# Eight shared groups moved beside the last sums, and rest tiles in a ring of six

## The reference

```
up_s   = einsum('th,seh->tse', xt, shared_up)            # 2 shared experts, 128 hidden
shared = einsum('tse,she->th', gelu(up_s), shared_down)
probs  = softmax(xt @ router_w.T);  topk_p, topk_i = top_k(probs, 4)   # of 16 experts
act    = gelu(einsum('th,reh->tre', xt, routed_up)) * gate
routed = einsum('tre,rhe->th', act, routed_down)
out    = x + shared + routed
```

## Time and profile before

| | us |
|---|---|
| median of 3 runs | 2615.87 (2613.97 to 2619.16) |
| the profiled execution: time | 2607.09 |
| its span | 2605.3 |
| PE / DVE / ACT / POOL busy in the span | 2062.6 / 1587.6 / 1255.6 / 1218.3 |
| SP's first load of the sums, last sum's store issued | 2350.8, 2601.9 |

### The profile page before, as it was taken

How to read it: one execution, slowest core, us unless ns; L and a number is a source line. 1 busy time by engine, 2 the same in 40 slices (tenths; PEclk the granted TensorE clock), 3 DMA queues, 4 the chain that set the end, 5 groups by cost and what they waited for, 6 DMA issues and landing times. The chain is left out here.

```text
span 2605.3 us, 55887 instructions
## 1 busy us (share of the span) xinstructions
PE 2062.6 (79%) x20646; PEld 1553.4 (60%) x20646; DVE 1587.6 (61%) x4387; ACT 1255.6 (48%) x2364; POOL 1218.3 (47%) x1648
## 2 busy tenths in 40 slices
PE   5889898989889898888888789999999998970000
PEld 3656565656666666666565567787778777760000
DVE  3566666666666666665666346666666666654666
ACT  3454544454545455454544346666666666650000
POOL 1034444444434443434444637777777767770000
PEclk8999999999999999999999799999999999995555
DMA  8254545545454545453544467777777777759999
GB/s 263 82 162 145 175 151 164 165 149 175 147 172 146 172 143 175 142 175 126 170 139 160 175 219 242 255 240 247 259 259 242 256 260 241 262 194 373 411 413 358
DMA packets 373934, 547.32 MB, mean 210 GB/s; under 512 B 100385, under 2 KB 306210, under 8 KB 369570
## 3 DMA queue, kind: packets, MB, share of 16 engines
q1 hardware_dynamic: 321634, 393.20, 46.5%
q0 software_dynamic: 52032, 150.54, 15.3%
HBM read 241.12 MB, written 302.52 MB: 209 GB/s over the span
## 5 line engine op out<-in xcount | busy, mean ns | idle before, releaser
L1050 POOL DMA_INDIRECT xs<-xn,idx x512 | 503.3, 983 | 601.9 <-DVE xn L907 157.7
L1075 POOL DMA_INDIRECT yt<-yo,ix x572 | 552.9, 967 | 225.7 <-issue 144.0
L671 ACT ACTIVATE pr<-A 128x512 f32<-128x512 f32 x512 | 264.4, 602 | 396.8 <-PE A L505 396.8
L802 DVE TENSOR_REDUCE ms<-A 128x4 f32<-128x512 f32 x512 | 316.6, 680 | 75.4 <-PE A L481 74.4
L627 PE MATMUL A<-wt,hh 128*128 128x256 f32 x1144 | 244.2, 296 | 0.7 <-DVE hl L952 0.7
L941 DVE TENSOR_TENSOR xl<-A,xh 128x512 fp32r<-128x512 f32 x286 | 183.3, 681 | 100.7 <-ACT xh L722 100.5
L585 PE MATMUL A<-ident,xr 128*128 128x128 f32 x1400 | 187.6, 278 | 63.5 <-DMA xr<-xs 31.1
L585 PEld LDWEIGHTS A<-ident,xr 128*128 128x128 f32 x1400 | 161.2, 142 | 115.6 <-DMA xr<-xs 42.9
L540 PE MATMUL A<-wos,ot 128*128 128x256 f32 x512 | 164.9, 450 | 79.8 <-ACT ot L680 79.8
L501 PE MATMUL A<-qt,km 32*128 32x128 f32 x4096 | 219.7, 333 | 0.6 <-DVE mt L822 0.6
L501 PEld LDWEIGHTS A<-qt,km 32*128 32x128 f32 x4096 | 183.9, 211 | 54.1 <-issue 49.8
(11 more groups left out here) (145 smaller groups left out, 4098.9 us busy)
## 6 DMA issues: line engine op xcount, KB each, us to landing
xr<-xs SPq DMA_DIRECT2D x143, 576.0 KB, 5.1
xs<-empty SPq DMA_DIRECT2D x36, 2048.0 KB, 10.7
gb<-yt SPq DMA_DIRECT2D x32, 2048.0 KB, 16.1
xb<-in_x SPq DMA_DIRECT2D x32, 512.0 KB, 6.6
cg<-in_ctx_t SPq DMA_DIRECT2D x32, 512.0 KB, 4.0
yd<-xb SPq DMA_DIRECT2D x32, 512.0 KB, 3.2
x2d<-xn SPq DMA_DIRECT2D x32, 512.0 KB, 3.0
xr<-x2d SPq DMA_DIRECT2D x32, 512.0 KB, 4.6
```

The lines of the kernel that those rows point to most:

```text
L671: ac(pr[:, 4 * b:4 * b + 4, :].rearrange("p h s -> p (h s)"), banks[4 + b][:, :], ACT.Exp, scale=SCALE)\
L802: v.reduce_max(ms[n % 2][:, b, 0:4], banks[b][:, :].rearrange("p (h t) -> p h t", h=4), AX.X)\
L1050: q.indirect_dma_start(xs, bass.IndirectOffsetOnAxis(ap=idx[:, n, k:k + 1], axis=0), x2[g % 4][:, i, :], None).then_inc(sent[g % 4], 16)
L1075: q.indirect_dma_start(yt, bass.IndirectOffsetOnAxis(ap=ix[:, n % 8, k:k + 1], axis=0), yo[n % 4][:, k, :], None).then_inc(put[n % 4], 16)
```

## The change

`LATE = 8`. The shared groups 24 to 31 are no longer spread between the routed blocks: they are the last eight units, behind block 142. The other 18 are spread anew, one after every seven or eight blocks.

The sums become steps of the same lists. `OPEN`, behind the down matmuls of the last block, waits for the scatters and the stores to `yd` and loads four `gb` and six `rr` tiles. `SUM` steps stand behind the down matmuls of each late group. They follow `ORDER`: 0, 1, 2, 3, 24, 4, 5, 25, 6, 7, 8, 26, 9, 10, 11, 27, 12, 13, 28, 14, 15, 16, 29, 17, 18, 19, 30, 20, 21, 31, 22, 23. A late group has no `yr` tile: DVE adds its down matmuls' result into the `rr` tile that its sum uses, and nothing is stored to `yd`. On DVE this add stands ahead of the sums of that step (two or three early groups and then its own). `rr` is a ring of six; `xr` is moved behind `xl` in memory, so that the six tiles lie over `wt`, `xh` and one `xl`, which the late groups don't use. SP loads the `rr` of place f + 5 behind a wait for the store of place f - 1.

```diff
+LATE = 8
-    rest = G - AHEAD
+    rest = G - AHEAD - LATE
...
-        while g < G and (g - AHEAD + 1) * NT <= (t + 1) * (rest + 1):
+        while g < G - LATE and (g - AHEAD + 1) * NT <= (t + 1) * (rest + 1):
...
-    return out
+    return out + [("S", n) for n in range(G - LATE, G)]
...
+ORDER = sorted(range(G), key=lambda g: ((g + 1) / (G - LATE) if g < G - LATE else (g - G + LATE + 1.5) / (LATE + 1), g))
...
             out.append(("DN", u - 1))
+            if UNITS[u - 1] == ("R", NT - 1):
+                out.append(("OPEN", 0))
+            if u - 1 >= NU - LATE:
+                upto = ORDER.index(UNITS[u - 1][1])
+                while done <= upto:
+                    out.append(("SUM", done))
+                    done += 1
...
+        rr = [es.enter_context(nc.sbuf_tensor(f"rr{k}", [P, GT, E], F32)) for k in range(6)]
...
-                if kind == "S":
+                if kind == "S" and n < G - LATE:
...
+            def OPEN(_):
+                for k in range(4):
+                    sp.wait_ge(put[k], 16 * GT * len(range(k, NT, 4)))
+                for k in range(2):
+                    sp.wait_ge(yr_kept[k], 16 * ((G - LATE) // 2))
+                for f in range(6):
+                    if f < 4:
+                        load_gathered(f)
+                    load_rest(f)
+
+            def SUM(f):
+                sp.wait_ge(added, f + 1)
+                sp.dma_start(token_rows(out, ORDER[f]), rr[f % 6][:, :, :]).then_inc(stored[f % 6], 16)
+                if f + 4 < G:
+                    load_gathered(f + 4)
+                if f > 0 and f + 5 < G:
+                    sp.wait_ge(stored[(f - 1) % 6], 16 * ((f - 1) // 6 + 1))
+                    load_rest(f + 5)
...
-                    dve.wait_ge(yr_in[n % 2], 16 * (n // 2 + 1))
+                    if n < G - LATE:
+                        y = yr[n % 2]
+                        dve.wait_ge(yr_in[n % 2], 16 * (n // 2 + 1))
+                    else:
+                        f = ORDER.index(n)
+                        y = rr[f % 6]
+                        dve.wait_ge(rr_in[f % 6], 16 * (f // 6 + 1))
```

More of the change, by code:

```diff
@@ L89, in ffn_steps @@
 def ffn_steps():
-    out, up = [], 0
+    out, up, done = [], 0, 0
     for u in range(-2, NU + 1):
@@ L103, in ffn_steps @@
             out.append(("DN", u - 1))
+            if UNITS[u - 1] == ("R", NT - 1):
[5 more added lines that the diff above has]
+                    done += 1
         if u + 2 < NU and UNITS[u + 2][0] == "R":
             out.append(("WC", UNITS[u + 2][1]))
-    return out
+    return out + [("SUM", f) for f in range(done, G)]
 ATT = attention_steps()
@@ L215, in sc @@
             return late.enter_context(nc.sbuf_tensor(name, shape, dt))
-        xr = [sc(f"xr{k}", [P, GT, W]) for k in range(3)]
         wt = [sc(f"wt{k}", [P, 2, 2, E], F32R) for k in range(3)]
@@ L220, in program @@
         xl = [sc(f"xl{k}", [P, KC, T], F32R) for k in range(2)]
+        xr = [sc(f"xr{k}", [P, GT, W]) for k in range(3)]
         xf = [sc(f"xf{k}", [P, KC, T]) for k in range(2)]
@@ L231, in program @@
         gb = [es.enter_context(nc.sbuf_tensor(f"gb{k}", [P, GT, TOPK, E], F32)) for k in range(4)]
-        rr = [es.enter_context(nc.sbuf_tensor(f"rr{k}", [P, GT, E], F32)) for k in range(4)]
+        rr = [es.enter_context(nc.sbuf_tensor(f"rr{k}", [P, GT, E], F32)) for k in range(6)]
         banks = [es.enter_context(nc.psum_tensor(f"A{b}", [P, 512], F32)) for b in range(8)]
@@ L255, in program @@
         put = [sem(f"put{k}") for k in range(4)]
-        gb_in, rr_in = [sem(f"gb_in{k}") for k in range(4)], [sem(f"rr_in{k}") for k in range(4)]
-        add_done, added, stored = sem("add_done"), sem("added"), [sem(f"stored{k}") for k in range(4)]
+        gb_in, rr_in = [sem(f"gb_in{k}") for k in range(4)], [sem(f"rr_in{k}") for k in range(6)]
+        add_done, added, stored = sem("add_done"), sem("added"), [sem(f"stored{k}") for k in range(6)]
         block = es.enter_context(nc.Block())
@@ L375, in DN @@
                     sp.dma_start(token_rows(yd, n), yr[n % 2][:, :, :]).then_inc(yr_kept[n % 2], 16)
-                    if 0 < n < G - 1:
+                    if 0 < n < G - LATE - 1:
                         sp.wait_ge(yr_kept[(n - 1) % 2], 16 * ((n - 1) // 2 + 1))
@@ L386, in TR @@
                     load_unit(u + 3)
[L388 to L396, removed]
-                             yt[g * P * GT * TOPK:(g + 1) * P * GT * TOPK, :].rearrange("(p r) e -> p (r e)", p=P))\
-                    .then_inc(gb_in[g % 4], 16)
@@ L400, in load_rest @@
[L400 to L413, removed]
@@ L414, in _, with load_gathered, load_rest @@
-            for k in range(4):
-                sp.wait_ge(stored[k], 16 * (G // 4))
+            def load_gathered(f):
+                g = ORDER[f]
+                sp.dma_start(gb[f % 4][:, :, :, :].rearrange("p i k e -> p (i k e)"),
+                             yt[g * P * GT * TOPK:(g + 1) * P * GT * TOPK, :].rearrange("(p r) e -> p (r e)", p=P))\
+                    .then_inc(gb_in[f % 4], 16)
+            def load_rest(f):
+                sp.dma_start(rr[f % 6][:, :, :], token_rows(yd, ORDER[f])).then_inc(rr_in[f % 6], 16)
@@ L417, in _ @@
+            run(FFN, {"TR": TR, "DN": DN, "OPEN": OPEN, "SUM": SUM})
+            for k in range(6):
+                sp.wait_ge(stored[k], 16 * len(range(k, G, 6)))
         @block.tensor
@@ L966, in DN, with SUM @@
                 else:
-                    dve.wait_ge(yr_in[n % 2], 16 * (n // 2 + 1))
+                    if n < G - LATE:
[5 more added lines that the diff above has]
+                        dve.wait_ge(rr_in[f % 6], 16 * (f // 6 + 1))
                     for k, b in enumerate(own):
                         wait_filled(dve, b, "DN", u)
-                        y2 = yr[n % 2][:, 2 * k:2 * k + 2, :].rearrange("p q e -> p (q e)")
+                        y2 = y[:, 2 * k:2 * k + 2, :].rearrange("p q e -> p (q e)")
                         v.tensor_tensor(y2, banks[b][:, :], y2, ALU.add).then_inc(drain[b], 1)
-            run(FFN, {"TR": TR, "U": U, "DN": DN})
-            for g in range(G):
-                p = g % 4
+            def SUM(g):
+                p, h = g % 4, g % 6
                 dve.wait_ge(gb_in[p], 16 * (g // 4 + 1))
-                dve.wait_ge(rr_in[p], 16 * (g // 4 + 1))
+                dve.wait_ge(rr_in[h], 16 * (g // 6 + 1))
+                if ORDER[g] >= G - LATE:
+                    u = UNITS.index(("S", ORDER[g]))
+                    for b in FFN_BANKS["DN"](u):
+                        wait_drained(dve, b, "DN", u)
                 pair = [gb[p][:, :, k:k + 2, :].rearrange("p i k e -> p i (k e)") for k in (0, 2)]
@@ L981, in _ @@
                 dve.wait_ge(add_done, 2 * g + 1)
-                v.tensor_tensor(rr[p][:, :, :], rr[p][:, :, :], gb[p][:, :, 0, :], ALU.add).then_inc(add_done, 1)
+                v.tensor_tensor(rr[h][:, :, :], rr[h][:, :, :], gb[p][:, :, 0, :], ALU.add).then_inc(add_done, 1)
                 dve.wait_ge(add_done, 2 * g + 2)
-                v.tensor_tensor(rr[p][:, :, :], rr[p][:, :, :], gb[p][:, :, 1, :], ALU.add).then_inc(added, 1)
+                v.tensor_tensor(rr[h][:, :, :], rr[h][:, :, :], gb[p][:, :, 1, :], ALU.add).then_inc(added, 1)
+            run(FFN, {"TR": TR, "U": U, "DN": DN, "SUM": SUM})
         @block.gpsimd
```

## The result

The changed kernel takes 2588.88 us (median of 6 runs, 2583.81 to 2594.46) against 2612.36 for the kernel before in the same comparison. The ratio is 0.9916, 95% interval 0.9895 to 0.9936: 17 to 27 us less. The forecast was 26.4 us less.

The account below looks back on a forecast made before the run. The prediction took GpSimd to bound the expert stretch and the DMA queue the last; -40 + 2.6 + 7 + 4 = -26.4 us, taken off the median 2615.87, gave 2589 us, with 8 in 10 in 2568 to 2610.

Parts of the forecast that it names:

- GpSimd bounds the expert stretch: Expert stretch: GpSimd, at 5.25 us a routed block, sets the pace despite TensorE's 91%; 143 blocks take 750.5 us.
- 40 us from the waits: Routed stretch: with eight groups gone, GpSimd's 54 us of waits shrink, gaining 40 us (bounds 17 and 54).
- a balance of 26.0 against 26.25 us between two five-block groups: Routed stretch: over five blocks and a shared group PE needs 26.0 us, GpSimd 26.25, leaving nothing for PE's load waits.
- The rival that gave the waits to the group itself: Routed stretch: PE's 9.2 us between outputs around a group makes GpSimd wait; gain only 3 us, 2613; chance 12%.
- the price of the six-block groups (0.73): Routed stretch: each of the 18 remaining groups costs GpSimd 0.73 us of waits, 13 us in all.
- Two moved loads, 2.6 us: Last stretch: two x2d loads of late groups stand behind the opening on SP, adding 2.6 us.
- The opening, 7 us: Start of the sums: DVE's first late add waits for rr tile 4, the queue empties about 7 us (bounds 4 and 10).
- Inside the ring, 4 us: Last stretch: late adds four places apart each leave the DMA queue empty 1 us, four times, adding 4 us.
- The ring of six gives nothing: Last stretch: the deeper ring of rest tiles adds no gain, because the DMA queue is already full.
- the rival that it makes the queue faster: Last stretch: the longer ring lifts the rate from 412 to 430 GB/s, 10 us less, 2579; chance 12%.
- PE's late work is hidden: Last stretch: PE's 15 us a late group fits into 3 or 4 sums, at least 22.9 us, adding nothing.
- The rival of the empty queue: Last stretch: each of eight late adds empties the queue 9.0 us, 72 instead of 11, giving 2651; chance 6%.

Follow-up runs that it names:

- experiment 6: The kernel before with half of each shared group's up matmuls left out (output not the reference's); 2589.16 us, ratio to before 0.9929.
- Experiment 1: The changed kernel with its 18 early shared groups at the old spacing of five or six blocks; 2608.66 us, ratio to before 1.0009.
- experiment 9: The kernel before with xr in a ring of four, rows loaded four units ahead, no group moved; 2566.33 us, ratio to before 0.9809.
- late4: sums_first with four late groups (LATE = 4), 22 shared groups staying in the routed stretch; 2583.60 us, ratio to before 0.9888.
- sums_first: The changed kernel with each step's early sums put ahead of the late group's add on DVE and SP; 2567.09 us, ratio to before 0.9857.
- xr4_late4: late4 with xr in a ring of four, rows loaded four units ahead; 2564.08 us, ratio to before 0.9802.
- xr4: sums_first with xr in a ring of four, rows loaded four units ahead; 2558.16 us, ratio to before 0.9797.
- experiment 3: The changed kernel with only sums 0 to 3 put ahead of the first late add; 2583.22 us, ratio to before 0.9894.

## Why the prediction was right, and where not

*GpSimd bounds the expert stretch: right.* Its pace of 5.25 us a block was the floor of every kernel. The nearest came to 752.6 us against 750.5; 60 us less of PE's work in the changed kernel shortened the stretch by 36.8, and the 45 us of experiment 6 by 17.4.

*40 us from the waits: right in size (36.8), right only in part in its mechanism.* Experiment 1 shows that spacing counts beside number. The reason that I gave, a balance of 26.0 against 26.25 us between two five-block groups, is the step that failed. It would leave the kernel before without a way to fewer waits at its own spacing, and with four xr tiles it has 5.1 us of them (experiment 9). PE as a whole has 26 us to spare; what it lacks with three tiles is the freedom to use them. A unit's load stands behind GpSimd's payload copy of the unit three before (SP stands there for 619 of the 750 us of experiment 9's last line; with four tiles it does so for 594, but a unit earlier), PE waits for the load while GpSimd is busy, and then a shared group comes with too little finished output in hand.

How much is in hand can be read from the traces. I call lead the time from DVE's last write of a block's yo tile to GpSimd's first scatter from it. The lead of the last block ahead of a shared group, as a mean over the groups but the first, goes with GpSimd's waits over 0.4 us, divided by the number of groups:

| kernel (experiment) | lead ahead of a group, us | waits a group, us |
|---|---|---|
| before | 3.9 | 2.1 |
| crowded (1) | 4.0 | 1.9 |
| late4 (7) | 4.5 | 1.6 |
| before_half_up (6) | 4.8 | 1.5 |
| after | 5.6 | 1.0 |
| sums_first (2) | 5.8 | 0.6 |
| xr4_late4 (10) | 6.4 | 0.4 |
| xr4_before (9) | 6.7 | 0.2 |
| xr4 (8) | 9.2 | 0.1 |

In every one of them a group takes 4.7 to 4.8 us of the lead where enough is there, and about 0.8 us is the least that is left behind one. So a group that finds less than some 5.5 us makes GpSimd wait. The rival that gave the waits to the group itself had this piece right: the group takes its share whatever the spacing, and a cheaper up product (experiment 6) doesn't change it. What it missed is that the lead ahead of the group can be raised.

Wider spacing, cheaper groups and a deeper ring each raise it; the deeper ring does nearly all of it. For the same reason the price of the six-block groups (0.73) was too low for a rule: 22 groups at six or seven blocks cost 1.6 each (with the doubt named there), 18 at seven or eight 1.0 in the changed kernel and 0.6 in sums_first, whose routed part is the same. That spread is the size of what one profile can say.

*Two moved loads, 2.6 us: right.* With the six-tile ring and the sums in front, the last stretch is 254.6 us with eight late groups and 251.1 with four or none. All loads of four are ahead of the opening. 3.5 us are the two loads and all else that eight groups bring. In xr4 only one of the two loads is left behind the opening, and its last stretch is 253.3 us, 1.3 less than that of sums_first, which is what one load was reckoned at.

*The opening, 7 us: right.* 6.2 us by the rate between 2347 and 2359, 6.3 by experiment 3. The first late add came 30.2 us after the first load, forecast 28.

*Inside the ring, 4 us: the mis-sized term.* It measured 11.7. The places were right, the four steps of four, and the price wrong: 3 us each instead of 1. I had set one sum's traffic against one add, one sum and a start-up, and counted only the time in which nothing is left to move. The trace has the times as reckoned: DVE is released at 2413.57, SP issues next at 2419.61, and the last tile that lay in the queue lands at 2421.21, so the queue is hardly ever empty. What I had left out is that a queue which has run low, and is being filled again, is slow as well. At 2420 some 3 MB are in flight where 5 to 8 are usual, and until 2430 the engines are busy 97% of the time and move 320 GB/s; a packet of 16 KB takes 757 ns in the mean there, 611 in the ten us behind. DVE's work doesn't slow them: DVE is as busy between 2570 and 2580 (9.86 of 10 us), at 422 GB/s. Nor does PE's, which has none between 2540 and 2550, at 338. A queue that has run low is what the slow windows share; no run changes that alone, so why it is slow stays open. The term made the last stretch 272.6 instead of 268.

*The ring of six gives nothing: 3.5 us off,* and the rival that it makes the queue faster isn't borne out: the middle of the stretch keeps its rate. The gain is the shorter end.

*PE's late work is hidden: right.* Last stretches with and without it differ by 3.5 us, all of which the moved loads may be. *The rival of the empty queue* has its mechanism shown by experiment 2, at 18.0/8 = 2.3 us a group, under the 4.7 from which it would have decided. *The tail* didn't show: the last scatters of the changed kernel follow each other with 0.30 us between them, and the first load of the sums is issued 1.7 us after the end of the last one, 1.6 before.

In sum, 36.8 us were won and 18.0 given back, 18.8 net in the profiles where 26.4 were forecast: 3.2 less won, 4.4 more lost. The times say 23.5, and the forecast is inside their 17 to 27. That 2589 met 2588.88 to the microsecond is luck: the kernel before came out 3.5 us lower with more runs, and the gain 3 us smaller. In the last stretch too two errors partly cancel, 7.7 us too little for the ring's places and 3.5 too much by giving the six tiles nothing. What the experiments add is that the part given back can be kept (experiment 2), and that the won part needed no move at all (experiment 9): xr4_before and xr4 differ by 3 us in their ratios, which their intervals don't resolve, and by 4.4 us in the two stretches.

## What to carry to other kernels

A producer that is faster on average but lumpy, as PE is here beside GpSimd, needs look-ahead rather than less work: before moving lumps out of its way, count how many units ahead its inputs are loaded and what that load waits for; one more tile did here what moving eight groups did, at a fraction of the rewriting. And where work is put into a stretch whose queue is full, its place in the in-order engine matters more than its length: a 1.3 us add that waits for a far tile, put ahead of work whose tiles had landed, cost 6 us once and about 3 us four times, and put behind that work at most 1 us in all (3.5 us, of which 2.6 are moved loads).

## What the runs showed of the hardware that I had not expected

A queue that is full at 412 GB/s drains in one gap of issuing: SP issued nothing for some 11 us, and the rate over 12 us fell to 198 GB/s. And it need not run empty to lose: while it filled again from some 3 MB in flight, the DMA engines showed 94 to 97% busy at 314 to 338 GB/s, so their busy share didn't tell the loss. Each scatter of GpSimd kept its 1.27 us whatever else ran (752.6 us for 572 of them and 143 payloads in the fastest kernel, 1.1 us of it waits). And profiles of kernels alike up to that point put the first scatter up to 9.6 us apart; 6.1 us of this are why the spans of the two profiles differ by less than the medians.
